# Four graph layers on one core: the transposes of two 1024x1024 matrices read as fp32r in place of fp32

## The reference

```
x = ln(x + groups_of_25_nodes(x, adj))                          # layer 0
z = x @ W.T + bW                                                # layer 1, graph attention
e = leaky(ai[:, None] + aj[None, :]);  att = where(adj > 0, e, MASKED)
x = ln(x + softmax(concat([att, SINK]))[:, :n] @ z)
x = ln(x + relu(((1 + eps2) * x + adj @ x) @ W12 + b12) @ W22 + b22)          # layer 2
h = rmsnorm((eps3 * x + adj @ x) @ W13 + b13) * rms_w                         # layer 3
x = ln(x + silu(h) @ W23 + b23)
```

## Time and profile before

| | |
|---|---|
| median of 3 runs | 2746.48 us (2746.43 to 2747.16) |
| the profiled execution | 2746.2 us, its span 2744.4 us |
| TensorE (PE) busy | 2644.1 us, 96%, 14650 instructions |
| VectorE (DVE) busy | 2022.4 us, 74% |
| ScalarE (ACT) busy | 1561.2 us, 57% |
| GpSimd (POOL) busy | 1277.7 us, 47% |
| TensorE's granted clock, mean | 0.988 of full speed |
| transposes of `att` (L896) and of `adj_col` (L910) | 1024 each |

### The profile page before, as it was taken

The page is one execution under the profiler, slowest core; times in us unless marked ns, Lnnn a source line. Parts: engine busy times, 40 slices in busy tenths (PEclk is TensorE's granted clock), DMA queues, the critical chain, the costliest instruction groups (busy, mean ns, idle before and its releaser), DMA issues.

```text
span 2744.4 us, 41122 instructions
## 1 busy us (share of the span) xinstructions
PE 2644.1 (96%) x14650; PEld 2267.5 (83%) x14650; DVE 2022.4 (74%) x4504; ACT 1561.2 (57%) x2911; POOL 1277.7 (47%) x1384
## 2 busy tenths in 40 slices
PE   6499999999999999999999999999999999999997
PEld 5478888888888888888888888888888888888986
DVE  5776877868687786868878686786868778686735
ACT  2437557464755756466565646656475575647524
POOL 2243554535455354545635454553635545354533
PEclk9799999999999999999999999999999999999998
DMA  7030402204040120403113040220404022040200
GB/s 225 18 127 1 154 1 77 77 3 152 1 130 25 59 96 1 154 1 109 46 39 116 1 154 1 89 66 23 132 1 154 1 82 74 8 146 1 78 1 16
DMA packets 205224, 181.00 MB, mean 66 GB/s; under 512 B 17367, under 2 KB 186718, under 8 KB 205022
## 3 DMA queue, kind: packets, MB, share of 16 engines
q1 hardware_dynamic: 197454, 177.04, 20.1%
q10 hardware_dynamic: 7568, 1.34, 0.3%
HBM read 161.15 MB, written 17.19 MB: 65 GB/s over the span
## 4 chain that ended last, share of the span: by engine, by line
PE 89%; ACT 3%; DVE 3%; issue 1%; POOL 0%; ACTq 0%; POOLq 0%; DVEq 0%
PE bank L945 13%; PE bank L949 13%; PE bank L946 12%; PE bank L1024 9%; PE bank L1010 8%; PE bank L995 6%; PE bank L996 6%; PE bank L1000 6%; PE bank L1028 4%; PE bank L910 4%; PE bank L896 4%; PE bank L975 3%; PE bank L1042 1%; ACT att L1205 1%; PE bank L923 1%
## 5 line engine op out<-in xcount | busy, mean ns | idle before, releaser
L945 PE MATMUL bank<-mt_hi,x_hi 128*128 128x512 f32 x1536 | 630.2, 410 | 0.3 <-ACT x_hi L1196 0.3
L949 PE MATMUL bank<-mt_hi,x_lo 128*128 128x512 f32 x1536 | 602.3, 392 | 0.0
L946 PE MATMUL bank<-mt_lo,x_hi 128*128 128x512 f32 x1536 | 600.5, 391 | 0.0
L1370 POOL TENSOR_TENSOR rstd<-ve,neg_half 128x4 f32<-128x4 f32 x126 | 160.9, 1277 | 411.6 <-DVE ve L1546 410.0
L949 PEld LDWEIGHTS bank<-mt_hi,x_lo 128*128 128x128 f32 x1536 | 289.1, 188 | 63.8 <-POOL x_lo L1375 0.2
L945 PEld LDWEIGHTS bank<-mt_hi,x_hi 128*128 128x128 f32 x1536 | 289.9, 189 | 54.3 <-ACT scratch L1241 4.2
L946 PEld LDWEIGHTS bank<-mt_lo,x_hi 128*128 128x128 f32 x1536 | 290.6, 189 | 50.2
L1606 DVE TENSOR_TENSOR sq_sum<-sq_sum,scratch 128x512 f32<-128x512 f32 x224 | 154.7, 691 | 228.8 <-ACT scratch L1241 228.8
L995 PE MATMUL bank<-a_hi,W_lo 128*128 128x512 f32 x768 | 318.3, 414 | 2.9 <-ACT hid L1222 2.9
L996 PE MATMUL bank<-a_hi,W_hi 128*128 128x512 f32 x768 | 301.6, 393 | 0.0
L1169 ACT ACTIVATE mt_hi<-bank 128x512 fp32r<-128x512 f32 x256 | 153.0, 598 | 236.0 <-PE bank L910 236.0
(11 more groups left out here) (168 smaller groups left out, 6092.2 us busy)
## 6 DMA issues: line engine op xcount, KB each, us to landing
att<-in_adj SPq DMA_DIRECT2D x128, 512.0 KB, 7.9
adj_col<-in_adj SPq DMA_DIRECT2D x256, 256.0 KB, 3.0
out<-x_even SPq DMA_DIRECT2D x64, 128.0 KB, 2.8
out<-x_odd SPq DMA_DIRECT2D x64, 128.0 KB, 2.7
x_odd<-in_x SPq DMA_DIRECT2D x56, 128.0 KB, 4.3
x_even<-in_x SPq DMA_DIRECT2D x49, 128.0 KB, 3.8
G<-in_L_gnn_W SPq DMA_DIRECT2D x2, 2048.0 KB, 19.2
W_raw<-in_L_gnn_W SPq DMA_DIRECT2D x2, 1024.0 KB, 9.7
```

The lines of the kernel that those rows point to most:

```text
L945: nc.tensor.matmul(dst[:], hi, mt_hi[:, k, cols], start=k == 0, stop=False)
L946: nc.tensor.matmul(dst[:], hi, mt_lo[:, k, cols], start=False, stop=False)
L949: mm = nc.tensor.matmul(dst[:], lo, mt_hi[:, k, cols], start=False, stop=done)
```

## The change

The transposes of L896 and L910 get all three operands as fp32r. `att_r` is a second name for the bytes of `att`; for the adjacency `mt_lo`, which is fp32r and has the bytes of `adj_col`, is read directly; the PSUM bank is written through a bitcast; the identity is copied once into an fp32r tile `ident_r` by GpSimd. All other transposes (weights, layer 0, the row of aj, the rms factors) stay in fp32. What ScalarE and VectorE read from the bank stays as it was.

```diff
+        with ExitStack() as place:
+            att_r = sb("att_r", [P, NT, NODES], F32R, place)
         att = sb("att", [P, NT, NODES])
+        ident_r = sb("ident_r", [P, P], F32R)
...
                 nc.gpsimd.affine_select(out=ident[:], in_=ident[:], compare_op=ALU.not_equal, fill=1.0, base=0,
                                         pattern=[[-1, P]], channel_multiplier=1).then_inc(s_ident, 1)
+                pool.wait_ge(s_ident, 4)
+                nc.gpsimd.tensor_copy(ident_r[:], ident[:])
                 nc.gpsimd.memset(H_all[:], 0.0).then_inc(s_pad, 1)
...
-                        mm = nc.tensor.transpose(turn_bank[i][:, j * P:(j + 1) * P],
-                                                 att[:, 4 * i + j, k * P:(k + 1) * P], ident[:])
+                        mm = nc.tensor.transpose(turn_bank[i][:, j * P:(j + 1) * P].bitcast(F32R),
+                                                 att_r[:, 4 * i + j, k * P:(k + 1) * P], ident_r[:])
...
-                src = adj_col[:, k, half_cols(h)]
+                src = mt_lo[:, k, half_cols(h)]
                 for j in HALF_TILES:
                     cols = slice(j * P, (j + 1) * P)
-                    mm = nc.tensor.transpose(turn_bank[i][:, cols], src[:, cols], ident[:])
+                    mm = nc.tensor.transpose(turn_bank[i][:, cols].bitcast(F32R), src[:, cols], ident_r[:])
```

More of the change, by code:

```diff
@@ L95, in adj_resnorm @@
         s_l0_stored = sem("layer0_stored")
-        graph0 = (att, x_even, sq_sum, stat0, mv0, ve, rstd, qi, qj, ai, aj)
+        graph0 = (att, att_r, ident_r, x_even, sq_sum, stat0, mv0, ve, rstd, qi, qj, ai, aj)
         graph0_sems = (s_att_in, s_stats0, s_aggr0, s_var0, s_rstd0, s_y0, s_sums, s_ai, s_aj, s_l0_stored)
@@ L115, in prologue @@
              eps2, L2_W1, L2_b1, L2_W2, L2_b2, eps3, L3_W1, L3_b1, rms_w, L3_W2, L3_b2, x_l0):
-    att, x_even, sq_sum, stat0, mv0, ve, rstd, qi, qj, ai, aj = graph0
+    att, att_r, ident_r, x_even, sq_sum, stat0, mv0, ve, rstd, qi, qj, ai, aj = graph0
     s_att_in, s_stats0, s_aggr0, s_var0, s_rstd0, s_y0, s_sums, s_ai, s_aj, s_l0_stored = graph0_sems
```

## The result

The changed kernel takes 2726.9 us (median of 4 runs, 2724.53 to 2730.77) against 2746.45 us of the kernel before on the same chip. The ratio is 0.993, with an interval of [0.9916, 0.9943]. The forecast was 2706 us: the time is in the range and on the forecast side, but the gain is 19.5 us where 40 were expected. It came out where rival (e) had it (0.08 to 0.09 us a transpose, 15 to 30 us). The profiled execution took 2724.5 us, 21.7 us less than that of before.

The account below looks back on a forecast made before the run. TensorE, busy 96% of the span, was taken to bound the kernel. 2048 transposes saving 0.043 us each give 88 us, of which 40 reach the end: 2746.2 - 40 = 2706 us, range 2681 to 2768 us.

Parts of the forecast that it names:

- rival (e): Half way: transposes at 0.08 to 0.09 us, part of the gain taken back, 2716 to 2731 us; chance 0.15.
- Transposes are on the path, at what they keep the next matmul away.: TensorE, L896 and L910: transposes cost what they occupy, 0.110 us each by instruction starts; TensorE is 89% of the chain.
- At 128 columns that is 0.067 us.: Step of one fp32r transpose on L896 and L910, down from 0.110 us, saving 88 us of TensorE time.
- The line through the fp32r widths: TensorE's fp32r matmuls of 512 and 256 columns: 0.41 ns a column plus 13 ns that don't shrink.
- The short load goes with being a transpose.: Transposes' weight loads on TensorE: 142 ns against 189 ns for fp32r matmuls; fp32r transposes were taken to keep the short one.
- Rival (a): Weight load is the floor, 0.112 us a transpose, 2750 us; or no change, 2746 us; chance 0.18 for both forms.
- rivals a, b: Fp32r transposes: a, long weight load, 0.112 us, +4 us, chance 0.18; b, fixed step, 0.120 us, +20 us, chance 0.18.
- Together 2.5 of 5.5 us a graph.: Share of TensorE's saving reaching the end, the rest lost to ScalarE and VectorE waits; 40 us over sixteen graphs.
- The cast on GpSimd costs nothing.: Prologue's one 128x128 identity cast on GpSimd hides in 13.0 us of idle time; otherwise 0.3 us.
- TensorE's busy share falls below 96%: Sign of being right: TensorE's busy share drops below the 96% it had before the change.
- waits of 2 to 3 us a graph: TensorE's waits for ScalarE's squares, VectorE's sums and layer 2's tiles grow to this, with 159.4 us between graphs.

Follow-up runs that it names:

- steps: Separate kernel without the graph layers, TensorE running blocks of 128 like instructions back to back; from start to start, fp32 transpose 0.109 us, fp32r 0.087 us.
- half_tiles: Changed kernel, but each of the 2048 transposes turns only 64 of its tile's 128 columns; 2713.12 us, ratio 0.9879 against the kernel before.
- gap_after_sums: Changed kernel with GpSimd's diagonal addition waiting until VectorE's first eight attention sums of the next graph are done; 2717.29 us, ratio 0.9893 against the kernel before.
- before_gap_after_sums: Kernel before the change with GpSimd's diagonal addition moved behind the eight attention sums by the same wait; 2743.22 us, ratio 0.9987.

## Why the prediction was half right

- **Transposes are on the path, at what they keep the next matmul away.** Right: TensorE's time fell, and the kernel became faster. The method by starts (to the second matmul behind, less one step) gave 0.089 us here and 0.087 in a long row without neighbours.
- **"At 128 columns that is 0.067 us."** This is the step that failed. The ends of the range, 0.067 and 0.120, held the value; the choice did not: 0.089 us. The line through the fp32r widths assumed that the operand type alone sets the rate. The runs show that the streaming hardly bounds an fp32r transpose any more (0.084 us with 64 streamed columns, 0.087 with 128); the number of weight columns does, the columns of the tile being turned (0.061 us with 64, 0.087 with 128). Whether it does so by the load is open. The saving was 0.021 and 0.018 us a transpose instead of 0.043, 40 us instead of 88.
- **"The short load goes with being a transpose."** Right, and it was the clue: the load row stayed at 142 ns. I used it only to rule out the long load's 0.112 us, and didn't ask what step the short load allows. Rival (a) had the right side, the weights, with the wrong cost; rival (e) had the right number, without a mechanism.
- **The long load, or a fixed step of 0.120 us (rivals a, b).** Refuted for transposes: the fp32r transposes of 128x128 in steps took 0.087 us. The fp32r matmul of the same shape did take 0.112 us, with the long load; a fixed 0.120 us is refuted for it too.
- **"Together 2.5 of 5.5 us a graph."** As a share about right: 0.45 forecast, 0.49 to 0.54 measured of 40 us, 0.42 of 81 in half_tiles. But that is in part luck, since errors of both signs cancel. By stretches (means of 13 graphs) the forecast kept 0.14 of the early turns, 0.64 of the late ones and 0.52 of the adjacency; measured are 0.5, 0.8 and 0.3. And the collision, which the forecast did not know of, took a part: with the addition moved in both kernels, the change gives 28.9 (gap_after_sums) - 3.6 (before_gap_after_sums) = 25.3 of 40 us, 0.63. Its reason was half right too. Late layer 3 gave back part at the sums behind it, the early turns were partly waited away at ScalarE, and VectorE's last stretch was the tightest, as written. But there it wasn't that VectorE was full: in 12 of 15 graphs one sum was stopped by a GpSimd instruction for 0.97 us. I had read busy shares and not the spread of durations of one line, which shows it at once (12 of 240 over 1 us before the change).
- **The cast on GpSimd costs nothing.** No run tried it apart, and the traces can't tell 0.3 us: the first turn of aj begins at 97.9 and 98.1 us in the two traces without it, and at 97.4 to 100.8 us in those with it.
- **"TensorE's busy share falls below 96%", waits of 2 to 3 us a graph.** Too much, from the same term: the share is 96% by the page, waits grew by 14.3 us, 0.9 a graph.

At the forecast share, 40 us of saving would be 18 us, against 19.5 measured. So the size of the step makes up all of the missing 20.5 us, given a share that came out right partly by luck.

## What to carry to other kernels

Here the faster operand type took only the streaming out of the way, and what was left went by the weight columns. Where a weight load hides just under the streaming (142 ns from issue to end with a step of 0.110 us here), don't carry the line of the streaming below it: allow for a floor in between until a row of a smaller step says otherwise. Before counting what a faster engine gains, look at the longest instance of each line of its neighbours as well as at the mean: a collision that hides in one engine's slack costs more once the slack is used (3.6 us before, 8 to 9.6 after), and moving one GpSimd instruction by 2 us was then worth nearly half as much as the change itself.

## What the hardware showed that was not expected

- An fp32r transpose follows its weight columns: 0.087 us with 128, 0.061 with 64. The number of streamed columns made 0.002 us of difference. Why an fp32r matmul of the same shape takes 0.112 us is not explained; its weight load is the longer one, too. The weight loads of steps (busy us, mean ns of one):

```profile
L93 PEld LDWEIGHTS bank<-ident_r,tile_r 128*128 128x128 f32 x128 | 11.1, 141 | 0.0
...
L95 PEld LDWEIGHTS bank<-ident,tile 64*128 64x128 f32 x128 | 8.2, 140 | 0.1
L101 PEld LDWEIGHTS bank<-ident_r,tile_r 128*64 128x64 f32 x128 | 7.8, 110 | 0.0
```

- With 64 streamed columns on 64 partitions the fp32r transpose (0.084 us) is slower than the fp32 one (0.064 us), though both load 128 weight columns. So the floor goes with the operand type as well; no run shows why.
- The granted clock fell to half, 1.2 GHz, in two rows of fp32r instructions that stream 64 columns, although TensorE was busy all the time, and rose again in the blocks behind. It did not fall in L95, with 64 fp32 columns, but L97 follows right behind L95, so which of the two led to the first fall isn't shown. Stretches of steps (length; busy us of PE, PEld, DVE, ACT, POOL; clock, third from the end, in shares of 2.4 GHz):

```profile
60.50:68.30 7.80, 7.80 (x126) 7.80 (x126) 0.00 (x0) 0.00 (x0) 1.00 0.01 2
...
68.50:70.30 1.80, 1.80 (x24) 1.80 (x22) 0.00 (x0) 0.00 (x0) 0.97 0.00 0
71.90:83.80 11.90, 11.90 (x95) 11.89 (x94) 0.00 (x0) 0.00 (x0) 0.50 0.01 1
86.00:99.30 13.30, 13.30 (x118) 13.06 (x117) 0.00 (x0) 0.00 (x0) 0.95 0.01 1
101.00:107.10 6.10, 6.10 (x105) 6.10 (x103) 0.00 (x0) 0.00 (x0) 1.00 0.01 3
126.00:145.60 19.60, 19.60 (x94) 19.60 (x93) 0.00 (x0) 0.00 (x0) 0.50 0.00 1
```

The first is L95, 64 fp32 columns streamed, at full clock. The next two are the beginning of L97 (64 fp32r columns) and what follows in it, the last is L105, also with 64 streamed columns. Their steps at half clock (0.127 and 0.213 us) are therefore not used above. In the changed kernel's stretches the clock stayed at 1.00.
